# Row maxima of the eight-wide self attentions taken for two heads at once, with the causal mask added on TensorE

## The chip, the cores and the metric

The kernel runs on one core of a Trainium2 chip. The metric is the device time of one execution in microseconds (us). TensorE (PE in the rows) multiplies matrices, VectorE (DVE) reduces and combines, ScalarE (ACT) applies functions and copies, GpSimd (POOL) does the rest, and SyncE (SP) issues transfers. Each engine works through its own instructions in the order in which the program wrote them, and waits on semaphores for the others.

## The reference, cut to what matters

A decoder of four layers is applied to x of 4 x 512 x 128 (batch, positions, channels). Each layer is a self attention, a cross attention and a feed-forward block, each with a residual and a layer norm behind it. The change touches the self attentions of layers 0, 1 and 3: 16 heads of width 8, 512 positions, with a causal mask in layers 0 and 1 and none in layer 3. Layer 0 has an additional branch on top, which the change leaves alone. In short:

```
q, k, v = split_heads(x @ Wq), split_heads(x @ Wk), split_heads(x @ Wv)   # 16 heads x 8
scores  = q @ k.T * 8 ** -0.5                                             # 512 x 512 for each head
scores  = where(causal, scores, -1e30)                                    # layers 0 and 1
out     = softmax(scores) @ v                                             # uses the maximum of each row
```

## The kernel before, in words

Two streams run through the same list of stages, each with two of the four batches, one after the other; the second stream lags the first by `LAG = 60` of the planned time units. Each stage is a set of steps with planned times. `weave` sorts the steps of both streams by these times for every engine, and that fixes the order in which the engine executes them. The planned times have no other effect: at run time an engine goes on as soon as its next instruction's semaphores allow. An instruction that waits therefore holds up both streams on its engine. Each stream has four PSUM banks of 512 float32 columns.

`attention8` computes the self attention of one batch in two phases. So there are twelve such attentions, eight of them causal.

*The ring* (the first phase) finds the row maxima, which the softmax subtracts. It goes over eight head pairs i. For each head pair TensorE builds a stack of keys and a stack of queries (L534, three 512-column bf16 matmuls each) in which the values are split into bf16 parts; ScalarE copies them to `KS` and `QS` (L619, L621). Head 2i lies on partitions 0 to 63 and head 2i+1 on 64 to 127. Then TensorE makes the scores of both heads for four blocks of 128 queries (L540, 64 rows of the array each, at row 0 or row 64), and VectorE takes their row maxima into `mx`. Without a mask this is a `tensor_reduce` (L693). With a mask, block j needs only the first 128 (j + 1) keys, and one `tensor_tensor_reduce` (L690, shown as a custom operation plus a short read of its accumulator) adds the mask from SBUF, writes the sum to a scratch tile `junk` (the tile `rest`) and keeps the maximum.

The steps of this phase share the four banks as a ring: step n uses bank n % 4 and waits (`freed(n - 4)`) until the step four before it has been read. The order is: stacks of pair 0, stacks of pair 1, scores of pair 0, stacks of pair 2, scores of pair 1, and so on: 16 stacks and 64 scores, planned 0.7 apart (D1), each reader 1.0 behind its writer.

*The second phase* makes the transposed scores (L554, "st"), their exponentials (L630, on ScalarE), the causal cut of the diagonal blocks (L663, on GpSimd), the product with the values (L564, "pv"), and every fourth time a turn of the output (L633, L570, L709, L710). TensorE's waits here are on ScalarE and GpSimd (L554 needs one of three banks free again, L564 needs the exponentials, cut where causal).

The first stream's ring runs beside whatever stage the second stream is in (at the start of the program beside nothing); the second stream's ring runs mostly beside the first stream's second phase. "Leading" and "lagging" rings below mean these two.

The lines in rows are those of the kernel before unless said otherwise.

## Time and profile before

| what | value |
|---|---|
| device time, three runs | 3488.41, 3495.7, 3497.16 us (median 3495.7) |
| the profiled execution: device time, span | 3504.39 us, 3502.2 us |
| mean granted TensorE clock | 0.831 of full speed |
| busy share: PE, DVE, ACT, POOL | 82%, 53%, 29%, 15% |
| chain that ended last, by engine | PE 64%, DVE 19%, ACT 7%, issue 6% |

The busy time of an engine is the time in which at least one of its instructions runs. Matmuls are pipelined and their ends are modelled, so the start times of matmuls say more than their durations: a 512-column bf16 matmul is shown as about 0.38 us long, while the next can start 0.21 us behind it. The chain of waits goes back from the last instruction to what released it each time. The engine whose work stands in the chain in some stretch is the one whose time counts there.

### The profile page before, as it was taken

The page shows a single profiled execution, that of the slowest core. Times are in us where ns is not written, and L with a number is a line of the kernel's source. Part 1 is how long each engine was busy: PE and PEld are TensorE (multiplying, and loading weights), DVE is VectorE, ACT ScalarE, POOL GpSimd, SP SyncE. Part 2 cuts the span into 40 slices and gives each one's busy share as a digit, 9 for nine tenths or more (in the row PEclk, how much of TensorE's full clock was granted, in tenths as well). Part 3 has the DMA queues.
Part 4 walks back from the last instruction along what each step waited for, and adds up shares of the span by engine and source line. Part 5 has one row for each costly group of instructions (what it writes and reads, how often), then busy time and mean ns, then how long its engine had stood idle before and what let it go on. Part 6 is the DMA issues. An engine that isn't in the chain of part 4 may idle for free.

```text
span 3502.2 us, 40399 instructions
## 1 busy us (share of the span) xinstructions
PE 2877.4 (82%) x14574; PEld 1566.3 (45%) x14625; DVE 1864.2 (53%) x4927; ACT 1025.8 (29%) x2060; POOL 519.7 (15%) x801
## 2 busy tenths in 40 slices
PE   6899998779987766898878999988799876678985
PEld 2235566424543443245523356563245434432554
DVE  5443324753565888625354433356446559875253
ACT  2431211254223101551234221113533331025520
POOL 1220000121101442000013100011211125410000
PEclk9998977989987878898679988877899787788975
DMA  4000000100000000000000000000001000000000
GB/s 154 2 1 1 1 1 1 46 2 14 24 24 1 1 24 25 1 2 28 34 7 2 1 0 1 1 23 24 2 19 31 13 1 1 25 25 1 1 4 3
DMA packets 16422, 49.65 MB, mean 14 GB/s; under 512 B 1761, under 2 KB 8801, under 8 KB 14434
## 3 DMA queue, kind: packets, MB, share of 16 engines
q1 hardware_dynamic: 15650, 45.79, 3.8%
q8 instruction: 118, 1.93, 0.2%
q10 hardware_dynamic: 576, 1.29, 0.1%
q14 instruction: 78, 0.64, 0.1%
HBM read 45.43 MB, written 1.05 MB: 13 GB/s over the span
## 4 chain that ended last, share of the span: by engine, by line
PE 64%; DVE 19%; ACT 7%; issue 6%; SPq 1%; POOL 1%; DMA 1%; ACTq 0%; DVEq 0%; POOLq 0%
PE psum L979 8%; PE psum L967 4%; PE psum L564 4%; PE psum L534 3%; DVE keep_s L2216 3%; PE psum L554 3%; PE psum L947 2%; PE psum L1497 2%; PE psum L726 2%; PE psum L1327 2%; PE psum L1789 2%; DVE fs_v_s L2078 2%; DVE mx_s L693 2%; ACT PT_s L630 2%; PE psum L801 2%
## 5 line engine op out<-in xcount | busy, mean ns | idle before, releaser
L630 ACT ACTIVATE PT_s<-psum 128x512 f32<-128x512 f32 (+3 forms) x768 | 340.4, 495 | 250.4 <-PE psum L554 247.2
L690 DVE CUSTOM_DVE_ANT_0 rest_s<-psum,packed_early 128x128 f32<-128x128 f32 (+3 forms) x512 | 226.8, 487 | 166.3 <-PE psum L540 164.2
L396 POOL TENSOR_SCALAR ve<-mv 128x4 f32<-128x4 f32 x48 | 14.4, 301 | 1891.1 <-DVE mv L386 1890.9
L2121 PE MATMUL psum<-packed_early,keep_s 128*128 128x128 f32 x1024 | 176.7, 331 | 132.4 <-DVE keep_s L2216 132.0
L1002 ACT ACTIVATE PT_s<-psum 128x512 f32<-128x512 f32 (+1 forms) x224 | 121.1, 592 | 444.9 <-PE psum L969 444.9
L554 PE MATMUL psum<-QS_s,KS_s 64*128 64x512 bf16 (+3 forms) x768 | 199.5, 354 | 51.8 <-DMA QS_s<-nmT_s 38.5
L540 PE MATMUL psum<-KS_s,QS_s 64*128 64x512 bf16 (+3 forms) x768 | 189.2, 363 | 54.6 <-DVE mx_s L693 29.2
L2078 POOL TENSOR_TENSOR buffer<-sim_s 128x1024 f32<-128x1024 f32 x80 | 188.5, 2368 | 239.3 <-DVE keep_s L2216 237.1
L2121 PEld LDWEIGHTS psum<-packed_early,keep_s 128*128 128x128 f32 x1024 | 146.7, 172 | 168.5 <-DVE keep_s L2216 156.3
L979 PEld LDWEIGHTS psum<-vaug0x_s,PT_s 128*128 128x128 f32 (+1 forms) x1280 | 192.1, 236 | 60.8 <-ACT PT_s L1002 46.9
L979 PE MATMUL psum<-vaug0x_s,PT_s 128*128 128x65 f32 (+1 forms) x1280 | 198.5, 320 | 24.0 <-ACT PT_s L1002 20.2
L564 PE MATMUL psum<-PT_s,vaug 128*9 128x512 f32 (+3 forms) x1536 | 172.7, 523 | 42.3 <-POOL PT_s L663 28.3
L663 POOL TENSOR_SCALAR_AFFINE_SELECT PT_s<-PT_s 128x128 f32<-128x128 f32 x512 | 145.2, 294 | 384.2 <-ACT PT_s L630 379.2
L693 DVE TENSOR_REDUCE mx_s<-psum 128x1 f32<-128x512 f32 x256 | 160.5, 682 | 72.4 <-PE psum L540 72.0
L554 PEld LDWEIGHTS psum<-QS_s,KS_s 64*128 64x128 bf16 x768 | 54.2, 96 | 249.0 <-ACT PT_s L630 129.7
L1042 DVE RECIPROCAL rd_s<-psum 128x4 f32<-128x4 f32 x96 | 17.0, 177 | 224.8 <-PE psum L979 224.8
L619 ACT ACTIVATE KS_s<-psum,packed_early 128x512 bf16<-128x512 f32 x96 | 65.8, 686 | 226.9 <-PE psum L534 224.3
L540 PEld LDWEIGHTS psum<-KS_s,QS_s 64*128 64x128 bf16 x768 | 51.3, 96 | 174.0 <-DVE mx_s L693 67.0
L967 PE MATMUL psum<-qT0x_s,kT0x_s 64*128 64x512 f32 (+1 forms) x320 | 123.6, 809 | 2.7 <-ACT nmT_s L995 2.7
L1021 DVE TENSOR_REDUCE mxm_s<-psum 128x1 f32<-128x512 f32 x128 | 84.6, 687 | 75.1 <-PE psum L947 74.8
L410 ACT COPY xT<-psum 128x512 f32<-128x512 f32 x44 | 25.7, 584 | 310.2 <-PE psum L404 310.2
L2216 DVE SCALAR_TENSOR_TENSOR keep_s<-buffer,thr_s 128x1024 f32<-128x1024 f32 x80 | 115.7, 1463 | 0.5
(437 smaller groups left out, 5361.6 us busy)
## 6 DMA issues: line engine op xcount, KB each, us to landing
buffer<-packed_experts SPq DMA_DIRECT2D x36, 384.0 KB, 3.3
buffer<-packed_moe SPq DMA_DIRECT2D x4, 2048.0 KB, 8.0
buffer<-packed_cross SPq DMA_DIRECT2D x4, 2048.0 KB, 8.4
buffer<-packed_product SPq DMA_DIRECT2D x4, 1024.0 KB, 4.8
packed_early<-packed_early SPq DMA_DIRECT2D x1, 2654.5 KB
raw_s<-packed_setup SPq DMA_DIRECT2D x1, 1840.0 KB, 7.2
packed_late<-packed_late ACTq DMA_DIRECT2D x4, 314.0 KB, 3.7
QS_s<-nmT_s SPq DMA_DIRECT2D x72, 8.0 KB
```

Source lines behind the costliest of these rows:

```text
L540: pe.matmul(bank[n % 4][:, 0:n_keys], QS[half(h), h // 2, j * P:(j + 1) * P], KS[half(h), h // 2, 0:n_keys], start=True, stop=True, tile_p ...
L554: pe.matmul(bank[u % 3][:, q0_of(c):T], KS[half(h), h // 2, c * P:(c + 1) * P], QS[half(h), h // 2, q0_of(c):T], start=True, stop=True, ti ...
L564: mm = pe.matmul(OUT[32 * i:32 * i + 9, q0_of(c):T], vaug[:, c, 4 * g + i, :], PT[:, u % 2, i, q0_of(c):T], start=(c == 0), stop=(c == KC ...
L630: a.activation(PT[:, u // 4 % 2, i, q0_of(c):T], bank[u % 3][:, q0_of(c):T], ACT.Exp, scale=scale).then_inc(exp_done.sem, 1)
L663: g_.affine_select(out=blk, in_=blk, compare_op=ALU.is_ge, fill=0.0, base=0, pattern=[[1, P]], channel_multiplier=-1).then_inc(exp_masked. ...
L690: v.tensor_tensor_reduce(junk[:, u % 2, 0:w], bank[n % 4][:, 0:w], s.w["causal"][:, T - w:T], 1.0, -3e38, ALU.add, ALU.max, mx[:, j, h:h + ...
L693: v.tensor_reduce(mx[:, j, h:h + 1], bank[n % 4][:], AX_X, ALU.max).then_inc(scores_read.sem, 1)
L967: pe.matmul(bank[o][0:rows, :], kT[half(o), i, k0:k0 + rows], qT[half(o), i, :], start=True, stop=False, tile_position=(64 * o, 0))
L979: mm = pe.matmul(O[o][:, j, :], PT[0:rows, u % 2, o, j * P:(j + 1) * P], vaug[0:rows, c, 2 * i + o, :], start=(c == 0 and j == 0), stop=(c ...
L2078: return eng.tensor_tensor(dst, m[:, 0, :].unsqueeze(2).to_broadcast([P, NK, NK]), m[:, 1, :].unsqueeze(1).to_broadcast([P, NK, NK]), ALU.add)
L2121: mm = pe.matmul(CT[:, c * P:(c + 1) * P], keep[:, n % KEPT, c * P:(c + 1) * P], s.w["ident"][:], is_transpose=True, start=(h == 0 and c % ...
L2216: v.scalar_tensor_tensor(keep[:, n % KEPT, :], fs, thr[:, j % 2, h:h + 1], fs, ALU.is_ge, ALU.mult).then_inc(kept.sem, 1)
```

## The change

1. The scores of the two heads of a pair, for one block of queries, become one step ("score" u // 2). TensorE waits until both banks are free (`freed(n - 4)` and `freed(n - 3)`), issues both matmuls, and signals once.
2. VectorE reads both banks in one `tensor_reduce` with two results. Its planned time is 1.0 behind the second of the two ring places; the matmuls' planned time is that of the first. So there are 32 reads for each attention instead of 64.
3. In the causal layers TensorE adds the mask to the diagonal block: a matmul of a bf16 identity (`ident16`) with a bf16 triangle of 0 and -1e30 (`causal16`), 128 columns, all 128 rows of the array, one for each head, accumulated onto the scores. The `tensor_tensor_reduce` with its scratch tile and its wait on the read before last goes away.
4. Two more constants of 128 x 128 bf16 are loaded in the setup.

```diff
+    c["ident16"] = np.eye(P, dtype=np.float32).astype(mybir.dt.np(BF16))
+    c["causal16"] = np.where(np.tril(np.ones((P, P))) > 0, 0.0, -1e30).astype(np.float32).astype(mybir.dt.np(BF16))
...
-        plan.append((T1 + D1 * n, kind, u))
-        plan.append((T1 + D1 * n + 1.0, "copy" if kind == "stack" else "max", u))
+        if kind == "stack":
+            plan += [(T1 + D1 * n, kind, u), (T1 + D1 * n + 1.0, "copy", u)]
+        elif u % 2 == 0:
+            plan += [(T1 + D1 * n, kind, u // 2), (T1 + D1 * (n + 1) + 1.0, "max", u // 2)]
...
-        return stacks_copied(u + 1) if kind == "stack" else scores_read(u + 1)
+        return stacks_copied(u + 1) if kind == "stack" else scores_read(u // 2 + 1)
+    def pair_scores(u, w):
+        b = slot[("score", 2 * u)] % 4
+        return s.psum[:, b:b + 2, 0:w]
...
-                h, j = scores[u]
-                pe.wait_ge(*stacks_copied(2 * (h // 2) + 2))
+                i, j = pairs[u]
+                n = slot[(kind, 2 * u)]
+                if n >= 4:
+                    pe.wait_ge(*freed(n - 4))
+                    pe.wait_ge(*freed(n - 3))
+                pe.wait_ge(*stacks_copied(2 * i + 2))
                 n_keys = (j + 1) * P if causal else T
-                pe.matmul(bank[n % 4][:, 0:n_keys], QS[half(h), h // 2, j * P:(j + 1) * P], KS[half(h), h // 2, 0:n_keys],
-                          start=True, stop=True, tile_position=(64 * (h % 2), 0)).then_inc(ring_ready.sem, 1)
+                for o in range(2):
+                    mm = pe.matmul(bank[(n + o) % 4][:, 0:n_keys], QS[half(o), i, j * P:(j + 1) * P], KS[half(o), i, 0:n_keys],
+                                   start=True, stop=not causal, tile_position=(64 * o, 0), skip_group_check=True)
+                if causal:
+                    for o in range(2):
+                        mm = pe.matmul(bank[(n + o) % 4][:, j * P:(j + 1) * P], s.w["ident16"][:], s.w["causal16"][:], start=False, stop=True,
+                                       skip_group_check=True)
+                mm.then_inc(ring_ready.sem, 1)
...
-                h, j = scores[u]
-                n = slot[("score", u)]
-                v.wait_ge(*ring_ready(n + 1))
-                if causal:
-                    w = (j + 1) * P
-                    if u >= 2:
-                        v.wait_ge(*scores_read(u - 1))
-                    v.tensor_tensor_reduce(junk[:, u % 2, 0:w], bank[n % 4][:, 0:w], s.w["causal"][:, T - w:T], 1.0, -3e38,
-                                           ALU.add, ALU.max, mx[:, j, h:h + 1]).then_inc(scores_read.sem, 1)
-                else:
-                    v.tensor_reduce(mx[:, j, h:h + 1], bank[n % 4][:], AX_X, ALU.max).then_inc(scores_read.sem, 1)
+                i, j = pairs[u]
+                v.wait_ge(*ring_ready(filled[("pair", u)]))
+                v.tensor_reduce(mx[:, j, 2 * i:2 * i + 2], pair_scores(u, (j + 1) * P if causal else T), AX_X, ALU.max).then_inc(scores_read.sem, 1)
```

The two places below are those on which the prediction rests. The first is the ring of the first stream's first attention, which runs alone: TensorE's order for one head pair, before. `parts` are the stacks' inputs, `KS` and `QS` the stacks, and x2 means twice in a row.

```order
L534 MATMUL psum<-parts_s_11_207,c_selk 128x512 x3
L534 MATMUL psum<-parts_s_11_207,c_selq 128x512 x3
L540 MATMUL psum<-KS_s_14_210,QS_s_13_209 128x128 x2
L540 MATMUL psum<-KS_s_14_210,QS_s_13_209 128x256 x2
L540 MATMUL psum<-KS_s_14_210,QS_s_13_209 128x384 x2
L540 MATMUL psum<-KS_s_14_210,QS_s_13_209 128x512 x2
L534 MATMUL psum<-parts_s_11_207,c_selk 128x512 x3
```

And the same place in the changed kernel, where L547, L558 and L562 are the stacks, the scores and the mask.

```order
L547 MATMUL psum<-parts_s_11_209,c_selk 128x512 x3
L547 MATMUL psum<-parts_s_11_209,c_selq 128x512 x3
L558 MATMUL psum<-KS_s_14_212,QS_s_13_211 128x128 x2
L562 MATMUL psum<-c_causal_15,c_ident_14 128x128 x2
L558 MATMUL psum<-KS_s_14_212,QS_s_13_211 128x256 x2
L562 MATMUL psum<-c_causal_15,c_ident_14 128x128 x2
L558 MATMUL psum<-KS_s_14_212,QS_s_13_211 128x384 x2
L562 MATMUL psum<-c_causal_15,c_ident_14 128x128 x2
L558 MATMUL psum<-KS_s_14_212,QS_s_13_211 128x512 x2
L562 MATMUL psum<-c_causal_15,c_ident_14 128x128 x2
L547 MATMUL psum<-parts_s_11_209,c_selk 128x512 x3
```

Behind every pair of 64-row score matmuls there are now two 128-row mask matmuls. The second place is a lagging causal ring (`_s_6_`, `_s_5_`) beside the first stream's second phase (L554 "st", L564 "pv"), on TensorE, before.

```order
L564 MATMUL psum<-PT_s_12_208,vaug 9x256 x4
L554 MATMUL psum<-QS_s_13_209,KS_s_14_210 128x128
L540 MATMUL psum<-KS_s_6_530,QS_s_5_529 128x256
L554 MATMUL psum<-QS_s_13_209,KS_s_14_210 128x128
L540 MATMUL psum<-KS_s_6_530,QS_s_5_529 128x256
L554 MATMUL psum<-QS_s_13_209,KS_s_14_210 128x512
L540 MATMUL psum<-KS_s_6_530,QS_s_5_529 128x384
L554 MATMUL psum<-QS_s_13_209,KS_s_14_210 128x512
L540 MATMUL psum<-KS_s_6_530,QS_s_5_529 128x384
L564 MATMUL psum<-PT_s_12_208,vaug 9x128 x4
```

The same place in the changed kernel (L577 "st", L587 "pv").

```order
L587 MATMUL psum<-PT_s_12_210,vaug 9x256 x4
L577 MATMUL psum<-QS_s_13_211,KS_s_14_212 128x128
L558 MATMUL psum<-KS_s_6_532,QS_s_5_531 128x256 x2
L562 MATMUL psum<-c_causal_15,c_ident_14 128x128 x2
L577 MATMUL psum<-QS_s_13_211,KS_s_14_212 128x128
L577 MATMUL psum<-QS_s_13_211,KS_s_14_212 128x512
L558 MATMUL psum<-KS_s_6_532,QS_s_5_531 128x384 x2
L562 MATMUL psum<-c_causal_15,c_ident_14 128x128 x2
L577 MATMUL psum<-QS_s_13_211,KS_s_14_212 128x512
L587 MATMUL psum<-PT_s_12_210,vaug 9x128 x4
```

The two scores have moved together, and the mask matmuls stand between them and the next "st" of the other stream. VectorE's order beside these steps is the same but for the merged reads.

## Rows read from the trace of the kernel before

**Rows 1.** Stages, busy time by engine: one lone, one lagging and three leading rings.

```profile
core 0: us, PE busy (x) PEld busy (x) DVE busy (x) ACT busy (x) POOL busy (x), PEclk, DMA share, GB/s
43.80:71.10 27.30, 24.99 (x110) 9.30 (x110) 25.87 (x122) 10.76 (x22) 1.63 (x2) 1.00 0.04 11
...
85.30:142.50 57.20, 45.37 (x328) 15.87 (x331) 30.66 (x132) 36.12 (x86) 21.83 (x68) 0.95 0.01 1
635.70:688.30 52.60, 45.07 (x256) 26.31 (x258) 40.46 (x161) 17.82 (x35) 6.99 (x7) 0.94 0.11 38
...
1335.20:1403.90 68.70, 50.86 (x223) 24.80 (x224) 59.95 (x93) 10.15 (x19) 10.84 (x9) 0.86 0.09 31
...
1727.50:1796.70 69.20, 50.03 (x165) 22.06 (x166) 49.37 (x176) 15.51 (x35) 3.09 (x5) 0.70 0.09 34
```

**Rows 2.** Chain of waits by line, stretches 85.3 to 142.5, 635.7 to 688.3, 1335.2 to 1403.9.

```profile
by line: PE psum L564 17.6%; issue 14.3%; ACT PT_s L630 13.6%; PE psum L534 13.0%; PE psum L554 7.3%; POOL PT_s L663 6.3%; PE psum L540 4.5%; ACT qk_s L633 3.9%; PE psum L570 3.5%; ACT QS_s L621 3.5%; PE psum L789 2.7%; ACT KS_s L619 2.4%; 
...
by line: issue 14.3%; PE psum L1687 14.0%; PE psum L534 9.6%; PE psum L540 9.4%; PE psum L1677 7.5%; PE psum L506 6.0%; DVE rest_s L690 5.6%; PE psum L1612 5.1%; PE psum L1599 2.7%; DVE mx_s L1640 2.5%; DVE mx_s L690 2.3%; DVE masked_s L163
...
by line: DVE mx_s L693 35.5%; DVE keep_s L2216 9.7%; PE psum L534 6.0%; issue 5.8%; PE psum L2097 5.3%; DVE fs_v_s L2078 5.2%; PE psum L540 4.9%; PE psum L2121 4.7%; DVE qk_s L674 3.2%; PE psum L519 2.7%; PE psum L506 2.5%; PE psum L511 2.4
```

**Rows 3.** Groups of VectorE by shape: busy and mean ns, idle time before and releaser.

```profile
L693 DVE TENSOR_REDUCE mx_s<-psum 128x1 f32<-128x512 f32 x256 | 160.5, 682 | 72.4 <-PE psum L540 72.0
...
L690 DVE CUSTOM_DVE_ANT_0 rest_s<-psum,packed_early 128x512 f32<-128x512 f32 x128 | 84.9, 685 | 3.7 <-PE psum L540 3.2
...
L1401 DVE TENSOR_REDUCE mx_s<-psum 128x4 f32<-128x308 f32 x128 | 55.1, 472 | 52.3 <-PE psum L1314 51.6
```

**Rows 4.** Timeline of VectorE in the lone ring, one head pair (start, us, what).

```profile
51.26 0.29 DVE L690 CUSTOM_DVE_ANT_0 rest_s<-psum,packed_early 128x128 f32<-128x128 f32 x1
...
51.77 0.42 DVE L690 CUSTOM_DVE_ANT_0 rest_s<-psum,packed_early 128x256 f32<-128x256 f32 x1
...
52.46 0.55 DVE L690 CUSTOM_DVE_ANT_0 rest_s<-psum,packed_early 128x384 f32<-128x384 f32 x1
...
53.41 0.69 DVE L690 CUSTOM_DVE_ANT_0 rest_s<-psum,packed_early 128x512 f32<-128x512 f32 x1
...
54.74 0.29 DVE L690 CUSTOM_DVE_ANT_0 rest_s<-psum,packed_early 128x128 f32<-128x128 f32 x1
```

**Rows 5.** The same timeline, TensorE and ScalarE, the stacks of one head pair.

```profile
49.59 0.82 PE L534 MATMUL psum<-parts_s,c_selk 128*128 128x512 bf16 x3
50.25 0.81 PE L534 MATMUL psum<-parts_s,c_selq 128*128 128x512 bf16 x3
50.45 0.69 ACT L619 ACTIVATE KS_s<-psum,packed_early 128x512 bf16<-128x512 f32 x1 [2.46 <-PE psum L534]
50.99 1.29 PE L540 MATMUL psum<-KS_s,QS_s 64*128 64x128 bf16 x6
51.10 0.58 ACT L621 CAST QS_s<-psum 128x512 bf16<-128x512 f32 x1
```

**Rows 6.** Timeline of TensorE in two lagging rings, causal and not.

```profile
109.75 0.23 PE L540 MATMUL psum<-KS_s,QS_s 64*128 64x128 bf16 x2
109.81 0.38 PE L554 MATMUL psum<-QS_s,KS_s 64*128 64x512 bf16 x2
...
111.13 0.66 PE L570 MATMUL psum<-packed_early,qk_s 128*128 128x128 f32 x4 [0.94 <-ACT qk_s L633]
...
3172.17 0.39 PE L540 MATMUL psum<-KS_s,QS_s 64*128 64x512 bf16 x1
3172.39 0.38 PE L554 MATMUL psum<-QS_s,KS_s 64*128 64x512 bf16 x1
3172.70 0.82 PE L534 MATMUL psum<-parts_s,c_selk 128*128 128x512 bf16 x3
```

**Rows 7.** Timeline of VectorE in a leading ring of layer 3.

```profile
1347.11 2.48 DVE L693 TENSOR_REDUCE mx_s<-psum 128x1 f32<-128x512 f32 x4 [0.90 <-PE psum L540]
1349.51 1.22 DVE L2078 TENSOR_TENSOR fs_v_s<-sim_s 128x1024 f32<-128x1024 f32 x1
1350.76 1.28 DVE L2216 SCALAR_TENSOR_TENSOR keep_s<-fs_v_s,thr_s 128x1024 f32<-128x1024 f32 x1
```

**Rows 8.** Groups of TensorE by line: busy and mean ns, idle before and releasers.

```profile
L540 PE MATMUL psum<-KS_s,QS_s 64*128 64x512 bf16 (+3 forms) x768 | 189.2, 363 | 54.6 <-DVE mx_s L693 29.2 <-DVE mx_s L690 22.6 <-ACT QS_s L621 0.9
```

**Rows 9.** Who waited for the tile of the row maxima, whole execution.

```profile
  PE psum L540: 51.8, 62
...
  PE psum L534: 8.1, 9
```

More of the change, by code:

```diff
@@ L464, in attention8 @@
         qk_projected=2, v_projected=1 if wv is not None else 0, qk_biased=2, rotated=2 if rope else 0, rope_chain=4 if rope else 0,
-        roped=2 if rope else 0, keys_split=4, queries_split=4, v_ready=1, ring_ready=len(ring), stacks_copied=H, scores_read=H * TJ,
+        roped=2 if rope else 0, keys_split=4, queries_split=4, v_ready=1, ring_ready=H + H // 2 * TJ, stacks_copied=H, scores_read=H // 2 * TJ,
         chain=6 + G, max_split=1, max_turned=1, max_copied=1, max_rows=16 * 6, st_ready=H * KC, exp_done=H * KC,
@@ L483, in attention8 @@
     rden = s.tile("rden", [P, TJ, 4])
-    junk = rest
     attT, oT = qk[:, 0, :], qk[:, 1, :]
@@ L487, in attention8 @@
     OUT = bank[3]
-    scores = [(2 * i + o, j) for i in range(H // 2) for j in range(TJ) for o in range(2)]
+    pairs = [(i, j) for i in range(H // 2) for j in range(TJ)]
+    filled = {}
+    for step in ring:
+        if step[0] == "stack":
+            filled[step] = len(filled) + 1
+        elif step[1] % 2 == 0:
+            filled[("pair", step[1] // 2)] = len(filled) + 1
     ST = {n: (n // (4 * KC), n // 4 % KC, n % 4) for n in range(4 * KC * G)}
@@ L525, in tensor @@
             yield t
-            if kind in ("stack", "score"):
+            if kind == "stack":
                 n = slot[(kind, u)]
@@ L529, in tensor @@
                     pe.wait_ge(*freed(n - 4))
-            if kind == "stack":
                 i, q = u // 2, 1 - u % 2
@@ L616, in scalar @@
                 n = slot[("stack", u)]
-                a.wait_ge(*ring_ready(n + 1))
+                a.wait_ge(*ring_ready(filled[("stack", u)]))
                 if q == 1:
@@ L682, in vector @@
             if kind == "max":
-                h, j = scores[u]
-                n = slot[("score", u)]
-                v.wait_ge(*ring_ready(n + 1))
-                if causal:
-                    w = (j + 1) * P
-                    if u >= 2:
-                        v.wait_ge(*scores_read(u - 1))
-                    v.tensor_tensor_reduce(junk[:, u % 2, 0:w], bank[n % 4][:, 0:w], s.w["causal"][:, T - w:T], 1.0, -3e38,
-                                           ALU.add, ALU.max, mx[:, j, h:h + 1]).then_inc(scores_read.sem, 1)
-                else:
-                    v.tensor_reduce(mx[:, j, h:h + 1], bank[n % 4][:], AX_X, ALU.max).then_inc(scores_read.sem, 1)
+                i, j = pairs[u]
+                v.wait_ge(*ring_ready(filled[("pair", u)]))
+                v.tensor_reduce(mx[:, j, 2 * i:2 * i + 2], pair_scores(u, (j + 1) * P if causal else T), AX_X, ALU.max).then_inc(scores_read.sem, 1)
             elif kind == "split":
                 by_parity = lambda t_: t_.rearrange("p j (g o) -> p j o g", o=2)
-                v.wait_ge(*scores_read(H * TJ))
+                v.wait_ge(*scores_read(len(pairs)))
                 link(v.tensor_scalar(mx[:], mx[:], -1.0, None, ALU.mult))
```

## The prediction

> **What bounds the kernel now.** I read four views, in this order. First the chain of waits by engine: TensorE holds 64% of it and VectorE 19%, so what a step costs depends on which of the two is late in its stretch. Second the busy times of the stretches in which the twelve rings lie [rows 1]. The lone ring (43.8 to 71.1) has VectorE busy 25.87 of 27.30 us. A lagging causal ring (85.3 to 142.5) has TensorE busy 45.37 of 57.20 us and VectorE 30.66. The leading rings lie between, and the leading ring of layer 3 (1335.2) has VectorE at 59.95 of 68.70 us. Third the chain by line in these stretches [rows 2]. In the lagging causal ring it is made of TensorE's lines (named ones alone 17.6 + 13.0 + 7.3 + 4.5 + 3.5 + 2.7 = 49%), issue (14%) and the exponentials; the row maxima do not appear among its rows. In the leading causal ring the TensorE lines named hold 54%, the maxima 8%. In the leading ring of layer 3 the maxima hold 35.5%. Fourth the timelines, for how far apart instructions start [rows 4 to 7].
>
> So the change shortens an engine that is in the chain in a few stretches, and lengthens the one that is in it in most.
>
> **VectorE: what goes.** In the lone ring the reads start, for two heads, 0.69 us (256 keys, 51.77 to 52.46), 0.95 (384, to 53.41) and 1.33 (512, to 54.74, with about 0.1 of waiting) apart; without waiting 0.21, 0.345, 0.475 and 0.61 for one read of 128, 256, 384, 512 keys, so 3.28 us for a head pair, in a cycle of 54.74 - 51.26 = 3.48 [rows 4]. That is about 0.00105 us a column and the rest fixed. A plain reduce of 512 starts every 0.60 us (four take 2.48, the last of them 0.68) [rows 3, 7]. A reduce of four groups of 77 columns (308 in all) takes 472 ns and one of 512 takes 682 [rows 3]: 210 ns for 204 columns, the same slope, so several groups in one read cost nothing extra. For two banks I get 0.33, 0.60, 0.87 and 1.13 us, 2.93 us for a head pair. Saved: 0.35 us for each of 64 causal head pairs, and 4 x (1.20 - 1.13) = 0.28 for each of 32 others: 31 us of VectorE in all, of which only what is in the chain counts. In the three leading causal rings beside other work, the chain holds about 4.2 us of maxima in the ring at 635.7 (5.6 + 2.3% of 52.6); I take that as the mean of the three, 12.6 us, times 0.35/3.28: -1.4 us. In the two leading rings of layer 3 it holds 24.4 us each, some 20 pairs, times 0.07: -2.8 us for both. The two lagging ones of layer 3: -1.
>
> **TensorE: the mask.** Three parts, for each of 256 causal pairs of scores (8 attentions x 32).
> - Going from 64-row to 128-row matmuls and back. Three 512-column matmuls take 0.66 us to the next of their kind (49.59 to 50.25), but 0.74 when a 64-row one follows [rows 5]; a 64-row one follows a 64-row one after 0.22 us, a 128-row one after 0.31 [rows 6]. So 0.08 to 0.09 a change, and the mask brings two: 0.17.
> - Two mask matmuls of 128 columns. A bf16 one on 128 rows is not in the trace. From below: two concurrent 64-row ones of 128 columns are followed by the next after 0.06 us (109.75 to 109.81). From above: four float32 ones of 128 columns take 0.66 us, of which 0.33 is the spacing of the first three, 0.11 each [rows 6]. I take 0.075, nearer to the bf16 row: 0.15 for two.
> - The scores themselves cost no less than before. Two heads use different halves of the array, and two such matmuls already run side by side (109.75 x2, 0.23 in all [rows 6]); over the program 768 x 0.363 = 279 us of them fit into 189.2 busy us [rows 8].
>
> Together 0.32 us a pair (0.28 to 0.40 with the bounds), 10.2 us a ring if all of it were exposed. It is hidden where TensorE would wait anyway, before "pv" for GpSimd's cut, or before "st" for an exponential. In the order of the changed kernel most masks stand directly ahead of an "st", whose exponential is what ScalarE waits for; a few stand ahead of a "pv". TensorE and issue hold 63% of the chain there [rows 2]; I take 60%: four lagging causal rings x 6.1 = +25 us. In the three leading ones TensorE is busy 45.07 of 52.60 and 50.03 of 69.20 us [rows 1]; I take 45%: +14 us. At a lower granted clock, 0.70 in the ring at 1727.5, the columns cost more, which I leave inside the range.
>
> **The ring itself: coarser steps.** A pair is now filled, read and freed as a whole, and there are two places instead of four. What is queued behind TensorE's wait is everything of both streams; behind VectorE's, the other stream's reads. In the lone ring I follow one head pair, with t = 0 where its first stack starts [rows 5]. That start now needs both reads of block 2 to be over; VectorE then has only block 3 to read, and is through at t = 1.00. Before, it had half of block 2 as well, 0.48 us more. TensorE is done with the stacks at 1.40 (49.59 to 50.99), the scores of block 0 and the masks follow with the second mask starting at 1.63, and a read starts 0.27 behind (50.99 to 51.26), at 1.90: VectorE stood for 0.90 us. Block 1 needs the banks of the stacks, which are free when the queries' copy ends, at 51.10 + 0.58 - 49.59 = 2.09; with scores and masks it is read from 2.69. Block 2 is read from 3.29, and ends 0.95 later, at 4.24; the next stack starts at 4.29. The cycle was 3.48 and becomes 4.29, 0.81 us more, for seven head pairs: +5.7 us. The leading rings of layer 3 have no mask, but the same gap: block 0 is ready at 1.40 + 0.27 + 0.21 = 1.88 against 1.00. In about half of these places a VectorE instruction of 1.2 us of the other stream fills it [rows 7]: 16 x 0.88 x 0.5 = +7 us. In lagging rings VectorE has slack, and I count nothing.
>
> **Setup.** Two more loads of 32 KB, 0.2 us at most.
>
> **Sum.** Against the profiled execution's own 3504.4 us: 25 + 14 + 5.7 + 7 - 1.4 - 2.8 - 1 + 0.2 = +46.7, which I round to +45, to 3549. The median of the runs is 8.7 us lower, so 3541.
>
> **The rivals.**
> 1. *The masks fall into waits.* TensorE in a lagging ring is idle 57.20 - 45.37 = 11.8 us [rows 1], as long as the ten that the masks take. If every mask stood before a wait, only the ring's coarser steps would be left, less VectorE's gain: 5.7 + 7 - 5.2 = +7, 3503. Against it: the chain in these stretches is on TensorE and issue for 63%.
> 2. *Faster: VectorE's reads hold TensorE up more than the chain shows.* TensorE stood 51.8 + 8.1 = 60 us before L540 and L534 for the maxima [rows 9]. If half of it goes with the shorter, merged reads, -30, and the masks leave +8, it comes to -22, 3474. It decides where a merged read ends before TensorE comes back to its banks, which is so only when more than 1.4 us of other TensorE work stands between; for it speaks that rings beside other work take 52 to 69 us where the lone one takes 27. Against it: more than half of TensorE's wait before L540, 29.2 of 54.6 us [rows 8], lies in layer 3, where a two-bank read saves only 0.07 us.
>    A rule by which pairs gain: the Trainium skill (TensorE: Matmul & The Clock Gate, Part 3: Packing small matmuls) has matmuls on different row groups start about 4 ns apart. Rows 6 and 8 show that most of them did so before.
> 3. *Worse.* The coarser steps also cost in the lagging rings, 0.5 us a head pair there (48 of them), and the masks are exposed to 80% at 0.36: 24 + 66 + 10 = +95, 3590.
> 4. *The change doesn't do what it says*: a read over two banks could run as two. Rows 3 speak against it (four groups, no extra cost); it would be inside rival 3.
>
> **How the numbers follow.** The forecast has 0.57, rival 1 0.18, rival 2 0.20, rivals 3 and 4 0.05. Within 0.3%, 10.5 us, is about what a measurement here can't tell from no change. Faster: rival 2 and 0.02 of rival 1, 0.22. The same: 0.11 of rival 1. Slower: the rest, 0.57 + 0.05 + 0.05 = 0.67. The likeliest case alone spans 3515 to 3575 (32 to 80% exposed, 0.28 to 0.40 a pair). The range for 8 in 10 reaches into rival 1 and half of rival 2 below, and towards rival 3 above: 3480 to 3585.
>
> **What would show it.** In the changed profile: 128 two-bank reads of 512 keys without a mask and 64 with one at about 1.22 us, none of the custom operation; mask matmuls 0.06 to 0.11 us apart and 0.31 or so behind a 512-column score; the lone ring some 33 us long instead of 27.3, with VectorE waiting about 0.9 us once a head pair; lagging causal rings 63 instead of 57 us. I am wrong if the lagging causal rings keep their 57 us, or if the leading rings become shorter.

## The result, and the profile after

| | before | changed |
|---|---|---|
| median of six runs | 3495.35 us (3488.41 to 3502.75) | 3518.12 us (3509.27 to 3523.4) |
| ratio | | 1.0059, 95% interval 1.004 to 1.0078 |
| profiled execution: device time, span, clock | 3504.39, 3502.2 us, 0.831 | 3523.4, 3521.2 us, 0.831 |

The change makes the kernel slower by 0.6%, 22.8 us in the medians. The forecast was slower by 45 us: the direction is right, the time is inside the range, and the size is about twice what was measured.

The groups of TensorE by line that answer to [rows 8]: L558 is the scores, L587 "pv", L562 the mask. Behind the name stand busy us and mean ns, then the idle time before the group and what ended it.

```profile
L558 PE MATMUL psum<-KS_s,QS_s 64*128 64x512 bf16 (+3 forms) x768 | 152.3, 358 | 77.0 <-DVE mx_s L708 66.7 <-ACT QS_s L644 9.1
...
L587 PE MATMUL psum<-PT_s,vaug 128*9 128x512 f32 (+3 forms) x1536 | 172.7, 523 | 30.0 <-POOL PT_s L686 16.7 <-ACT PT_s L653 7.7 <-DVE att L725 3.6
...
L562 PE MATMUL psum<-c_causal,c_ident 128*128 128x128 bf16 x512 | 76.6, 234 | 0.0
```

And the row of "pv" on the page of before:

```profile
L564 PE MATMUL psum<-PT_s,vaug 128*9 128x512 f32 (+3 forms) x1536 | 172.7, 523 | 42.3 <-POOL PT_s L663 28.3
```

Three things stand in them. The masks are 76.6 busy us, but the scores fell from 189.2 to 152.3, so TensorE's busy time rose by 20 us only (2877.4 to 2897.2 on the two pages). The idle time before the scores rose from 54.6 to 77.0 us. And the idle time before "pv" fell from 42.3 us to 30.0: some of the mask has taken the place of waiting.

The waits for the row maxima, which answer to [rows 9]:

```profile
  PE psum L558: 66.7, 66
...
  PE psum L547: 23.3, 23
```

TensorE waits 90.0 us for maxima instead of 59.9. The merged reads are as cheap as worked out, and VectorE waits more for TensorE. The reads of two banks of 512:

```profile
L708 DVE TENSOR_REDUCE mx_s<-psum 128x2 f32<-128x1024 f32 x192 | 229.4, 1217 | 88.9 <-PE psum L558 84.2 <-PE psum L562 4.6
```

The lone ring, one head pair (timeline of TensorE and VectorE), beside [rows 4, 5]:

```profile
48.39 0.43 DVE L708 TENSOR_REDUCE mx_s<-psum 128x2 f32<-128x256 f32 x1 [0.81 <-PE psum L562]
48.69 0.28 PE L558 MATMUL psum<-KS_s,QS_s 64*128 64x256 bf16 x2 [0.34 <-ACT QS_s L644]
48.91 0.28 PE L562 MATMUL psum<-c_causal,c_ident 128*128 128x128 bf16 x2
49.13 0.34 PE L558 MATMUL psum<-KS_s,QS_s 64*128 64x384 bf16 x2
49.23 2.69 DVE L708 TENSOR_REDUCE mx_s<-psum 128x2 f32<-128x512 f32 x3 [0.42 <-PE psum L562]
...
52.73 0.42 DVE L708 TENSOR_REDUCE mx_s<-psum 128x2 f32<-128x256 f32 x1 [0.81 <-PE psum L562]
```

The cycle is 52.73 - 48.39 = 4.34 us (forecast 4.29, before 3.48), and VectorE stands still for 0.81 and 0.42 us in it (forecast 0.90 and 0.46). Two masks and the change back take 0.22 us (48.91 to 49.13). The change ahead of them takes about 0.10: in the trace a mask starts 0.16 us behind a pair of 128 columns, where the next 64-row matmul starts after 0.06 [rows 6].

The stretches of the rings, in the columns and the order of [rows 1] (lone, lagging causal, leading causal, leading of layer 3, leading causal):

```profile
43.40:76.30 32.90, 26.23 (x172) 11.27 (x172) 23.33 (x32) 11.07 (x23) 1.76 (x2) 1.00 0.04 11
90.30:150.70 60.40, 53.86 (x388) 20.20 (x393) 28.20 (x42) 36.46 (x86) 21.82 (x69) 0.92 0.00 1
645.00:704.40 59.40, 51.90 (x318) 30.83 (x320) 38.03 (x71) 17.87 (x35) 7.03 (x7) 0.86 0.10 33
...
1354.50:1429.90 75.40, 49.90 (x223) 27.37 (x224) 58.05 (x63) 10.23 (x19) 10.51 (x9) 0.78 0.08 28
...
1753.60:1813.90 60.30, 44.01 (x226) 21.09 (x228) 46.02 (x84) 15.48 (x35) 3.06 (x5) 0.83 0.10 39
```

From the first start of a score matmul to the last, all twelve rings in the traces (us):

| | lone | lagging, causal | leading, causal | leading, layer 3 | lagging, layer 3 |
|---|---|---|---|---|---|
| before | 27.2 | 57.0, 57.7, 59.1, 56.3 | 52.5, 69.1, 56.4 | 68.6, 68.6 | 66.9, 66.9 |
| changed | 32.7 | 60.2, 59.6, 60.4, 59.6 | 59.3, 60.1, 59.3 | 75.3, 72.6 | 64.1, 63.8 |

The lone ring came as forecast. The lagging causal ones grew by 2.4 us in the mean where 6.1 were forecast. The leading causal ring at 1727.5 became 9 us shorter, with a granted clock of 0.83 instead of 0.70. That goes with the change and is not chance alone. In the traces of before, e2, e4 and e8, where the two heads' scores are separate in the causal layers, this ring takes 69.1, 64.3, 69.1 and 69.0 us (73.0 in e6, with masks); in those of the nine kernels that issue them together it takes 59.6 to 62.8. Near the same clock the two kinds lie closer: 64.3 us at 0.76 (e2), 61.9 at 0.75 (e1).

Added up by kind, the twelve rings account for the change. The two profiled spans differ by 19.0 us, the rings by 20.5 (sums are taken before rounding):

| term of the forecast | forecast, us | rings, changed less before, us |
|---|---|---|
| lagging causal (mask) | +25 | +9.6 |
| leading causal (mask, less VectorE's 1.4) | +12.6 | +0.6 |
| lone | +5.7 | +5.5 |
| leading, layer 3 (coarser steps, less 2.8) | +4.2 | +10.7 |
| lagging, layer 3 | -1 | -5.9 |

### The profile page after: what moved, and what is told of

It is laid out like the page before. It is cut to its first block, busy times and chain, and to the rows that moved or that the text cites. A ratio compares the mean times of both kernels' runs of the same rounds, so it can differ in the third digit from the quotient of the medians.

```text
span 3521.2 us, 39650 instructions
## 1 busy us (share of the span) xinstructions
PE 2897.2 (82%) x15076; PEld 1588.8 (45%) x15137; DVE 1833.9 (52%) x4031; ACT 1027.3 (29%) x2060; POOL 518.0 (15%) x801
## 4 chain that ended last, share of the span: by engine, by line
PE 66%; DVE 19%; ACT 7%; issue 5%; SPq 1%; DMA 1%; POOL 1%; ACTq 0%; DVEq 0%; POOLq 0%
PE psum L994 8%; PE psum L587 4%; PE psum L982 4%; PE psum L547 3%; DVE mx_s L708 3%; PE psum L577 3%; DVE keep_s L2231 3%; PE psum L962 2%; PE psum L1512 2%; PE psum L741 2%; PE psum L1342 2%; PE psum L1804 2%; DVE fs_v_s L2093 2%; PE psum L1800 2%; PE psum L816 2%
## 5 line engine op out<-in xcount | busy, mean ns | idle before, releaser
L708 DVE TENSOR_REDUCE mx_s<-psum 128x2 f32<-128x1024 f32 (+3 forms) x384 | 357.4, 953 | 267.3 <-PE psum L562 182.4
L577 PE MATMUL psum<-QS_s,KS_s 64*128 64x512 bf16 (+3 forms) x768 | 202.4, 354 | 45.2 <-DMA QS_s<-nmT_s 36.9
L2093 POOL TENSOR_TENSOR buffer<-sim_s 128x1024 f32<-128x1024 f32 x80 | 187.3, 2353 | 242.1 <-DVE keep_s L2231 239.8
L558 PE MATMUL psum<-KS_s,QS_s 64*128 64x512 bf16 (+3 forms) x768 | 152.3, 358 | 77.0 <-DVE mx_s L708 66.7
L587 PE MATMUL psum<-PT_s,vaug 128*9 128x512 f32 (+3 forms) x1536 | 172.7, 523 | 30.0 <-POOL PT_s L686 16.7
L577 PEld LDWEIGHTS psum<-QS_s,KS_s 64*128 64x128 bf16 x768 | 54.3, 95 | 241.6 <-ACT PT_s L653 112.0
L547 PE MATMUL psum<-parts_s,c_selk 128*128 128x512 bf16 x234 | 85.5, 471 | 41.4 <-DVE mx_s L708 23.3
L558 PEld LDWEIGHTS psum<-KS_s,QS_s 64*128 64x128 bf16 x768 | 42.4, 95 | 169.3 <-DVE mx_s L708 108.0
```

Of the source, the lines that this page charges most:

```text
L547: mm = pe.matmul(bank[n % 4][:], sel[:, w, i, :], parts[:, q, w, :], start=(w == 0), stop=(w == 2))
L558: mm = pe.matmul(bank[(n + o) % 4][:, 0:n_keys], QS[half(o), i, j * P:(j + 1) * P], KS[half(o), i, 0:n_keys], start=True, stop=not causal, ...
L577: pe.matmul(bank[u % 3][:, q0_of(c):T], KS[half(h), h // 2, c * P:(c + 1) * P], QS[half(h), h // 2, q0_of(c):T], start=True, stop=True, ti ...
L587: mm = pe.matmul(OUT[32 * i:32 * i + 9, q0_of(c):T], vaug[:, c, 4 * g + i, :], PT[:, u % 2, i, q0_of(c):T], start=(c == 0), stop=(c == KC ...
L708: v.tensor_reduce(mx[:, j, 2 * i:2 * i + 2], pair_scores(u, (j + 1) * P if causal else T), AX_X, ALU.max).then_inc(scores_read.sem, 1)
L2093: return eng.tensor_tensor(dst, m[:, 0, :].unsqueeze(2).to_broadcast([P, NK, NK]), m[:, 1, :].unsqueeze(1).to_broadcast([P, NK, NK]), ALU.add)
```

## The experiments

Each kernel was timed in five or more rounds beside the kernel before; ratios are to it. An interval is about 0.0013 to 0.0027 to either side, so most differences of two ratios are sure to about 0.0024, 8 us. The kernels of the experiments choose their case by constants; the cuts of code below are written out for the case and shortened, with ... for what is left out. Those without a mask in the maxima leave it out there alone: the exponentials are still cut.

| | what | ratio (95%) |
|---|---|---|
| changed | | 1.0059 (1.004 to 1.0078) |
| e1 | merged, no mask | 1.0038 (1.0023 to 1.0052) |
| e2 | merged reads in layer 3 only | 1.0012 (1.0 to 1.0025) |
| e3 | the change in the causal layers only | 1.0073 (1.0059 to 1.0087) |
| e4 | single scores, plain single reads | 0.9991 (0.9973 to 1.0008) |
| e5 | every mask twice | 1.0038 (1.0021 to 1.0056) |
| e6 | single scores, mask on TensorE | 1.0146 (1.0119 to 1.0173) |
| e7 | block 2 single | 1.0066 (1.0042 to 1.009) |
| e8 | as e4, merged in layer 3's lagging rings | 0.997 (0.9951 to 0.999) |
| e9 | masks of 16 columns | 1.0082 (1.0065 to 1.01) |
| e10 | merged scores and masks, single reads | 1.0029 (1.0015 to 1.0044) |
| e11 | merged scores, no mask, single reads | 0.9985 (0.9969 to 1.0) |
| e12 | e11 in the causal layers, e8 in layer 3 | 0.9991 (0.9976 to 1.0006) |

**e1, no mask** (diff on the changed kernel).

```diff
-                                   start=True, stop=not causal, tile_position=(64 * o, 0), skip_group_check=True)
-                if causal:
-                    for o in range(2): ... ident16, causal16 ...
+                                   start=True, stop=True, tile_position=(64 * o, 0), skip_group_check=True)
```

> The changed kernel without the 512 mask matmuls: the row maxima of the diagonal blocks are taken over unmasked scores (the cut of the exponentials stays). It has the merged reads and the coarser ring, and none of the two changes of tiling mode a pair. The changed kernel is 22.8 us over the kernel before, ratio 1.0059. Theory A (the price of a mask pair, 0.31 us or 80 us in all, was right, but only a quarter of it is exposed): about 20 us come back, ratio 1.000 (0.998 to 1.002). Rival B (60% of the mask is exposed as forecast, and the merged reads gain 25 us that the forecast had not): 48 us come back, ratio 0.992 to 0.994. Rival C (the mask is hidden nearly all, the loss is the coarser ring): ratio 1.004 to 1.006.

Only 0.0021, about 7 us, comes back, and by the intervals that can't be told from nothing. Theory A's 20 us and rival B's 48 are both too much; rival C is nearest, just under its lower end. But the trace of e1 has a surprise: its lone ring takes 36.2 us, longer than with the masks. The stretch, busy times and clock:

```profile
43.90:80.20 36.30, 26.42 (x110) 8.79 (x108) 22.88 (x31) 10.63 (x22) 1.14 (x2) 0.72 0.03 8
```

The granted clock is 0.72 where it was 1.00 with the masks, and three 512-column matmuls of a stack take 1.46 instead of 0.82 us. So e1 takes away the masks and part of the clock.

**e2 and e3, the layers apart.** The change in layer 3 only (e2), and in the causal layers only (e3): `paired` is made false for the other kind, with the steps of before.

> Merged reads in layer 3 alone; the causal layers have single scores and the tensor_tensor_reduce, as before the change. In the profiles the four rings of layer 3 changed by +6.7, +4.0 (leading) and -2.8, -3.1 (lagging). Theory A: the coarser ring costs the leading rings about 5 us each and the lagging ones gain 3 each, +4 to +5 in all, ratio 1.001. My forecast's own terms, +7 - 2.8 - 1 = +3, can't be told from that; a ratio under 0.999 would say that merged reads gain.

> The change in the causal layers alone (merged reads, mask on TensorE), single reads in layer 3. Theory A: what is left of the 22.8 us without layer 3, +18, ratio 1.005. If layer 3 had been the larger part, ratio 1.001 or 1.002.

Layer 3 costs +0.0012, 4 us (0 to 9 by the interval), where the forecast had +3: in the trace its leading rings take 75.3 and 72.5 us, the lagging ones 64.1 and 63.8. The causal layers cost 0.0073, over the 1.005 expected and a little over the whole change, which with e2 is more than 0.0059 but about what can't be told.

**e4, plain single reads** (diff on the kernel before).

```diff
-                if causal:
-                    ... tensor_tensor_reduce(junk, bank, causal) ...
-                else:
-                    v.tensor_reduce(mx[:, j, h:h + 1], bank[n % 4][:], AX_X, ALU.max).then_inc(scores_read.sem, 1)
+                v.tensor_reduce(mx[:, j, h:h + 1], bank[n % 4][:, 0:(j + 1) * P if causal else T], AX_X, ALU.max).then_inc(scores_read.sem, 1)
```

> The kernel before with one edit: in the causal layers VectorE takes the maximum of one head's unmasked scores by a plain tensor_reduce, in place of the tensor_tensor_reduce with the mask; four places in the ring as before. Reads start 0.60 instead of 0.61 us apart at 512 keys, so VectorE is no faster; what goes is the accumulator read and one wait. Theory A and rival C: ratio 0.999 to 1.000. If the custom operation or its waits cost something that the trace before hid, under 0.998. Beside e1 it shows what merging the reads costs or brings without any mask: theory A has e1 0 to 5 us above it from the coarser ring, rival B has e1 15 us or more below it.

No difference from before. Neither mask nor custom operation on VectorE cost anything that shows.

**e5, every mask twice, and e9, masks of 16 columns.**

```diff
e5:  for o in range(2) of the mask: twice
e9:  -   bank[(n + o) % 4][:, j * P:(j + 1) * P], ident16[:], causal16[:]
     +   bank[(n + o) % 4][:, (j + 1) * P - 16:(j + 1) * P], ident16[:], causal16[:, P - 16:P]
```

> The changed kernel with every mask matmul issued twice (-2e30 in place of -1e30, which no maximum sees): 512 more mask matmuls of 128 columns, 0.066 us apart at the full clock, so 256 x 0.13 = 34 us more of TensorE with no further change of tiling mode. If a tenth to a quarter of the mask is exposed, as e1 suggests (ratio 1.0059 with, 1.0038 without), it is +3 to +8 us on the changed kernel, ratio 1.007 to 1.008. If 60% is exposed, as my forecast had it, +20, ratio 1.0115. Were the masks hidden in all places but the clock held up by them, it would be 1.006 or less.

> The changed kernel with mask matmuls of the last 16 columns of the diagonal block in place of 128 (the maxima see the other columns unmasked). It keeps the two changes of tiling mode a pair and leaves out most of the columns; in the lone ring the granted clock should show whether a mask matmul of few columns holds it up. If what a mask costs is its change of mode, the ratio stays that of the changed kernel, 1.005 to 1.006. If columns cost as forecast (60% of 256 x 0.1 us), 15 us less, 1.0015. If the mask's columns hold the clock up, the lone ring falls to the lower clock as in e1 and takes 36 us or more, against 32.7.

Both go against every theory that charges for columns. From 16 to 128 to twice 128 columns the ratio falls, 1.0082, 1.0059, 1.0038; each step is at the edge of what can be told, the two together (0.0044) are clear. The lone ring shows where it comes from; the row of e9, busy times and clock:

```profile
43.50:79.10 35.60, 27.82 (x170) 12.02 (x170) 22.72 (x31) 11.10 (x22) 1.03 (x2) 0.86 0.03 10
```

And that of e5:

```profile
44.50:78.60 34.10, 30.27 (x234) 14.67 (x232) 23.55 (x31) 10.81 (x22) 1.71 (x2) 0.99 0.03 9
```

The clock there is 0.72 without masks, 0.86 with 16 columns, 1.00 with 128, 0.99 with twice 128. The lone ring itself, from first to last score, takes 35.4 us with 16 columns, 32.7 with 128 and 33.9 with twice 128. So e5's gain over the changed kernel lies elsewhere: its leading causal rings at 644 and 2368 take 56.4 us each at a clock of 0.97, where the changed kernel's take 59.3 at 0.86. That is 5.8 of the 7 us between the two. The mean clock of the whole execution says the same in every run: 0.822 to 0.827 with 16 columns, 0.831 to 0.838 with 128, 0.836 to 0.845 with twice 128. (Without masks, in e1, it is 0.827 to 0.831.) The mask's columns cost TensorE time and are paid back by longer stretches at the upper clock.

**e6, the mask with single scores** (the kernel before with a mask matmul behind each score, and plain reads).

> Single scores and single reads as before the change, with the mask on TensorE behind each score: 512 mask matmuls, and up to two changes of tiling mode for each of them, 512 x (0.17 + 0.066) = 121 us of TensorE at most, less where a score lay between 128-row work anyway. No merged reads and four places in the ring. The theory that the loss sits in the coarser ring (12 us, e1) and the mask is hidden for nine tenths: ratio 1.003 to 1.004. The forecast's 60% exposed: 1.015 or more.

The forecast's kind of cost does exist: against e4 the same 512 mask matmuls cost 0.0155, 54 us. They stand behind each single score now, with a change of mode for each. They also come between scores that ran side by side: in e4's trace the two heads' scores of a block start within 20 ns of each other in 133 of 384 cases, in e6's in 41. Which of the two costs more is not shown. The scores' row:

```profile
L572 PE MATMUL psum<-KS_s,QS_s 64*128 64x512 bf16 (+3 forms) x768 | 243.7, 356 | 39.3 <-DVE mx_s L722 38.0
```

243.7 busy us against 189.2 before and 152.3 changed. The expectation that four places in the ring would make it cheap (1.003 to 1.004) was wrong.

**e7, block 2 single** (the changed kernel, blocks 0, 1 and 3 merged in the causal layers).

> The changed kernel, but in the causal layers the two scores of block 2 (384 keys) are made, masked and read singly; the others and layer 3 stay merged. The next stack then needs only the first head's read of block 2, 0.48 us earlier, and the queries' stack the second. If the stop of VectorE at the stacks is what lengthened the lone ring (4.34 us a head pair instead of 3.48, by the start of the stacks behind the merged read of block 2), a head pair becomes about 0.4 us shorter there, less 0.06 for the longer read: the lone ring 30 us instead of 32.7. If something else lengthened it, it stays at 32 or 33 us. The whole time then falls by 2 to 5 us, ratio 1.005.

The lone ring falls from 32.7 to 30.8 us, most of the way to 30, as the late start of the stacks asks. The whole does not fall (1.005 was expected): the lagging causal rings took 63.0, 61.7, 63.0, 61.7 us instead of 60.2, 59.6, 60.4, 59.6. Each has eight more groups of mask, with eight more changes there and back; that these are the cause is not shown apart.

**e10 and e11, reads apart from scores** (diff on the changed kernel; e11 without mask as well).

```diff
-                v.tensor_reduce(mx[:, j, 2 * i:2 * i + 2], pair_scores(u, w), AX_X, ALU.max).then_inc(scores_read.sem, 1)
+                for o in range(2):
+                    v.tensor_reduce(mx[:, j, 2 * i + o:2 * i + o + 1], bank[(n + o) % 4][:, 0:w], AX_X, ALU.max).then_inc(scores_read.sem, 1)
```

> The changed kernel's TensorE order word for word (merged scores and masks, in all layers), but VectorE reads each head by itself, and each read frees its own bank. So the stack of keys may start half a read of block 2 earlier, as before the change, while the scores of a pair still wait for both. The theory that the coarser ring is what costs: the lone ring falls from 32.7 to about 30 us, the leading rings of layer 3 from 75 and 73 towards 71, and the whole from 1.0059 to 1.002 to 1.004. Rival: merged reads gain something that the ring hides, and it becomes slower than the changed kernel, 1.007.

> The same without any mask: merged scores, single plain reads, each freeing its bank. Beside e4 (single scores, single plain reads, 0.9991) it shows what issuing two heads' scores together is worth by itself: TensorE's busy time in score matmuls was 189 us single and 152 merged. If that counts, 0.993 to 0.996; if it is hidden, or given back in the wait for both banks, 0.998 to 1.001.

TensorE's order is that of the changed kernel (of e1 for e11), and only the reads differ. Both came out inside what was expected, e11 with its rival case (0.998 to 1.001: the cheaper issue gains nothing). e10's lone ring takes 31.2 us, where about 30 was expected, and its leading rings of layer 3 take 73.5 and 72.4 instead of 71. With e4 they take the change apart, one edit at a time:

| step | ratio from, to | us |
|---|---|---|
| plain reads in place of the masked ones on VectorE (e4) | 1, 0.9991 | -3 |
| the two heads' scores issued together (e4 to e11) | 0.9991, 0.9985 | -2 |
| the mask on TensorE (e11 to e10) | 0.9985, 1.0029 | +15 |
| one read for two banks (e10 to changed) | 1.0029, 1.0059 | +10 |

The first two can't be told from nothing. The mask's 15 us are 8 to 23 by the intervals (the medians of the two kernels' own runs lie 21 apart). Merging the reads without the mask costs 0.0053, 19 us (e11 to e1), but there the lone ring fell to the lower clock: 7.0 of the 19 us lie in it. The rings by kind, in us from the first start of a score matmul to the last (the leading causal ring near 1730 by itself):

| | lone | lagging causal, four | leading causal, two | the one near 1730 | leading, layer 3, two | lagging, layer 3, two |
|---|---|---|---|---|---|---|
| before | 27.2 | 230.2 | 108.9 | 69.1 | 137.2 | 133.8 |
| e4 | 26.4 | 232.0 | 111.6 | 69.1 | 137.2 | 133.8 |
| e11 | 29.2 | 233.2 | 107.5 | 61.0 | 143.6 | 127.6 |
| e10 | 31.2 | 243.8 | 112.0 | 62.3 | 146.0 | 128.2 |
| changed | 32.7 | 239.8 | 118.6 | 60.1 | 147.8 | 127.9 |
| e1 | 36.2 | 232.6 | 115.6 | 61.9 | 147.8 | 127.9 |

Each line is one trace, and between kernels with the same code in a ring (e4 and e8, leading causal) an entry can differ by 4 us with the granted clock. Issuing the scores together (e4 to e11) is not idle work: it shortens the ring near 1730 and the lagging ones of layer 3, lengthens the lone one and the leading ones of layer 3, and comes to nothing. The mask (e11 to e10) lies in the lagging causal rings, +10.6, and in the three leading ones, +5.9. Where it went otherwise stands in TensorE's idle time before "pv" (L602) and before the scores (L574), e11 and then e10:

```profile
L602 PE MATMUL psum<-PT_s,vaug 128*9 128x512 f32 (+3 forms) x1536 | 174.1, 527 | 37.4 <-POOL PT_s L701 26.5 <-ACT PT_s L668 7.7 <-DVE att L747 0.8
...
L574 PE MATMUL psum<-KS_s,QS_s 64*128 64x512 bf16 (+3 forms) x768 | 146.8, 357 | 99.8 <-DVE mx_s L726 87.2 <-ACT QS_s L659 11.5
...
L602 PE MATMUL psum<-PT_s,vaug 128*9 128x512 f32 (+3 forms) x1536 | 174.2, 528 | 29.3 <-POOL PT_s L701 16.7 <-ACT PT_s L668 7.6 <-DVE att L747 2.9
...
L574 PE MATMUL psum<-KS_s,QS_s 64*128 64x512 bf16 (+3 forms) x768 | 151.5, 356 | 85.7 <-DVE mx_s L726 76.6 <-ACT QS_s L659 7.2
```

**e8 and e12, a version faster than both.**

> A version meant to be faster than both: no mask in the maxima of the causal layers, single plain reads there (as e4, ratio 0.9991), and merged reads only in the rings of layer 3 of the second stream, the two lagging ones, which became 2.8 and 3.1 us shorter in the changed kernel and in e2. The leading ones, 4.0 and 6.7 us longer there, stay single. Expected: -6 us from the two rings, -2 from the plain reads, ratio 0.9975 (0.996 to 0.999). If the lagging rings' gain is given back by the stage behind them, 0.999 to 1.000.

> The two versions that were faster than the kernel before, together: in the causal layers no mask, the two heads' scores issued together and read singly (e11, 0.9985), in layer 3 merged reads in the second stream's rings alone and single scores in the first's (e8, 0.997). If the two gains are of different stretches they add: e11 has also the leading rings of layer 3 longer by 2 to 4 us, which go here, so 0.995 to 0.997. If the causal part of e11 gains nothing over e8's single scores: 0.997.

e8 is faster than the kernel before by 0.3% (0.1 to 0.5%), as expected. e12, for which 0.995 to 0.997 was expected, came out at 0.9991, no difference, so e8's gain is small and its interval just clears one; I would not build on more than "not slower".

## Why the prediction had the direction right and the size wrong

- *What held.* Slower, by the mask on TensorE and by the coarser ring: e10 against e11 and the changed kernel against e10 show both.
- *The lone ring*: 4.34 us a head pair against 4.29, VectorE's stops where they were put, the stretch 32.9 us against 33. e7 shortened it by shortening the wait that was named.
- *VectorE's price for two banks*: 1.13 us apart was forecast, and the trace has 1.11 to 1.13 where two such reads follow without a wait; three reads of 256, 384 and 512 keys take 2.69 us in a row, 0.60 + 0.87 and the last one's 1.22 make that sum.
- *The step that failed is the mask's term*, "lagging rings +25, leading +14", 39 us. Measured, the mask costs 15 us (e10 against e11), or 7 by the changed kernel against e1, whose lower clock in the lone ring hides part of it. The price of one pair by itself was right: about 0.10 us for the change ahead and 0.22 for two masks and the change back, where 0.32 was forecast. The exposed share was wrong. From e11 to e10, TensorE's busy time in the four lagging causal rings grows by 30.5 us and the rings by 10.6; in the three leading ones by 16.2 and 5.9. So about a third of the added work shows, not 60 or 45%. The rest fell into waits, and 20 of these 30 us stand in two of them over the program: TensorE's wait before "pv" for GpSimd fell from 26.5 to 16.7 us, the one before the scores for the maxima from 87.2 to 76.6. The clock was not what paid here, as the lagging rings have 0.88 to 0.90 in both traces. The share had been read from the chain's share of TensorE. The chain says whose work ended last, and not how much more work fits before it ends later: TensorE was idle 11.8 of 57.2 us in a lagging ring before, and 6.5 of 60.4 after. The waits of that stretch would have been the better measure.
- *The columns* were half of the forecast's price (0.15 of 0.32 us a pair). By e5 and e9 more of them cost no more time in the end, since the granted clock rises with them.
- *"The scores themselves cost no less than before"* was wrong too. They fell from 189.2 to 152.3 busy us, 37 us, half of the masks' 76.6. The reading behind the sentence does not bear it: that 279 us of durations fit into 189.2 busy us says little of matmuls side by side, as a 512-column one is shown about 0.38 us long while the next can start after 0.22. In the trace of before, the two heads' scores of a block start within 20 ns of each other in 130 of 384 cases, in the changed one in 306. In the order of before each score of a pair had its own wait in front, and a step of the other stream often stood between the two. The Trainium skill (TensorE: Matmul & The Clock Gate, Part 3: Packing small matmuls) has matmuls on different row groups start about 4 ns apart; in the changed trace the two of a pair start 3 to 6 ns apart in the head pair shown above. Yet e4 and e11 differ by nothing in time, so this did not make the whole faster. Against e6, where the masks part the scores, e10 is 41 us faster (0.0117); it has half as many changes of mode as well, so the saving's own share of this is not shown.
- *The ring's coarser steps* were forecast at 5.7 + 7, less 5.2 for VectorE: +7.5. Measured, issuing together and reading together cost 8 us with the mask (e4 to e11, e10 to changed) and 16 without (e4 to e1), and TensorE's waits for maxima grew by 30 us. Those waits come with the joint issue, not with the merged reads: they are 91.5 us already in e10. "In lagging rings I count nothing" is borne out: merging the reads changes the lagging causal rings by -4.0 us (e10 to changed) and -0.7 (e11 to e1). What was missed lies in the two leading causal rings, +6.5 and +8.1, at a lower granted clock, and in the leading ones of layer 3.
- *Layer 3 came out by luck.* +3 was forecast and +4 measured (e2), but the leading rings grew by 10.7 us where 4.2 were forecast, and the lagging ones shrank by 5.9 where 1 was. e11 has nearly all of that with single reads (+6.4 and -6.2 against e4), so it is the joint issue of the scores and its wait for two banks, more than the gap behind a merged read that was worked out.
- *The rivals.* Rival 1 (the masks fall into waits) named what happened to two thirds of the mask, and its 3503 us is 15 from the measured time, the forecast 23. Its full form, no mask exposed, is not what was measured. Rival 2, faster reads paying, is refuted by e11 against e1. Of the signs of being wrong, the lagging causal rings did not keep their 57 us, but one leading causal ring did become shorter.
- *Two sums do not come out.* Rival 3's terms add up to 100 and not to 95. The likeliest case's lower end, with 32% of 224 pairs outside the lone ring at 0.28 us, is 3523 and not 3515, so the measured 3518 lies below it.

What stays open: whether the mask's 15 us are all changes of mode. e9 against e1 (0.0044, 15 us of 256 x 0.17 = 44) speaks for that, but the clock differs between these two as well, 0.822 to 0.827 against 0.827 to 0.831. Why the granted clock was lower in e1's lone ring and not in e11's, neither of which has masks, is open too.

## What to carry to other kernels

A read that takes two buffers at once also frees them at once: before merging, follow the ring for one cycle and see what must cover the longest producer then. The chain tells which engine is late, and not how full it is; the price of added work on that engine must be weighed against its waits in the same stretch. When work of another tiling mode is moved to TensorE, put it in few groups: here the same 512 mask matmuls cost 54 us behind single scores and 15 us in twos, and their columns cost nothing that could be measured. To learn what each part of a change is worth, undo one part at a time; a total that fits can be two errors that cancel, as in layer 3.

## What the runs showed of the hardware

- A change between 64-row and 128-row matmuls costs 0.08 to 0.10 us each way at the upper clock, seen before the change [rows 5, 6] and in the masks.
- Two heads' score matmuls on the two halves of the rows start 3 to 6 ns apart when issued together, as in the head pair shown; within 20 ns in 306 of the changed kernel's 384 pairs.
- Taking matmuls away made a stretch longer. In the lone ring with merged reads TensorE stood still for part of each cycle; the granted clock stayed at its upper level (2.4 GHz) with 128-column masks (32.7 us) and fell to the lower one (1.2 GHz) for part of it with 16-column masks (35.4 us) and without (36.2 us). With single reads and no masks (e11) it stayed at the upper level (29.2 us). These are one trace each; over the whole kernel the mean clock was 0.822 to 0.827 with 16 columns, 0.831 to 0.838 with 128 and 0.836 to 0.845 with twice 128, over all runs of each.
- A VectorE maximum over two PSUM banks of 512 columns takes 1217 ns where one bank takes 682; from start to start it is 1.11 to 1.13 us against 0.60 for one bank.
